# Two attention layers in one kernel: every values group in split form, sums seeded by copies, values four steps behind the scores

## The reference, cut to what matters

```python
# layer 0: 64 inner channels, no scale
g, theta, phi = g_w @ x + g_b, theta_w @ x + theta_b, phi_w @ x + phi_b
y = softmax(theta.T @ phi, axis=-1) @ g.T
x = W_w @ y.T + W_b[:, None] + x
# layer 1: 128 channels
q, k, v = Wq @ x + bq, Wk @ x + bk, Wv @ x + bv
out = softmax((q.T @ k) / sqrt(128), axis=-1) @ v.T
x = x + out.T
```

## Time and profile before

| | us |
|---|---|
| median of the runs | 3249.24 |
| the profiled execution | 3248.75 |
| its span, first to last instruction | 3246.9 |
| TensorE matmuls busy | 3207.7 (99%) |
| GpSimd busy | 3025.7 (93%) |
| VectorE, ScalarE busy | 2091.7, 1897.9 |
| granted TensorE clock | 0.997 |

### The profile page before, as it was taken

How to read it: one execution, slowest core, us unless ns; L and a number is a source line. 1 busy time by engine, 2 the same in 40 slices (tenths; PEclk the granted TensorE clock), 3 DMA queues, 4 the chain that set the end, 5 groups by cost and what they waited for, 6 DMA issues and landing times. The chain is left out here.

```text
span 3246.9 us, 38831 instructions
## 1 busy us (share of the span) xinstructions
PE 3207.7 (99%) x13636; PEld 2198.4 (68%) x13636; DVE 2091.7 (64%) x3036; ACT 1897.9 (58%) x2473; POOL 3025.7 (93%) x1611
## 2 busy tenths in 40 slices
PE   8999999999999999999999999999999999999997
PEld 5555555557777775555777776555577777777775
DVE  5555555556777765555777776555577777777773
ACT  5555555556666655555666665555566666666665
POOL 6988999999999999999999999999999999999998
PEclk9999999999999999999999999999999999999999
DMA  1000000004665650000565664000067575657566
GB/s 52 26 21 26 23 27 26 27 23 94 136 137 117 145 103 27 27 27 27 104 142 119 139 134 101 17 26 27 27 132 141 119 147 115 126 120 144 120 136 120
DMA packets 91922, 271.45 MB, mean 84 GB/s; under 512 B 10192, under 2 KB 10192, under 8 KB 91728
## 3 DMA queue, kind: packets, MB, share of 16 engines
q0 software_dynamic: 55296, 201.35, 32.3%
q1 hardware_dynamic: 36432, 67.62, 6.8%
HBM read 50.83 MB, written 16.78 MB: 21 GB/s over the span
## 5 line engine op out<-in xcount | busy, mean ns | idle before, releaser
L924 DVE TENSOR_REDUCE piece_max<-rough 128x1 f32<-128x512 f32 x2032 | 1316.5, 684 | 707.0 <-PE rough L510 696.9
L1046 POOL TENSOR_TENSOR p_lo<-probs,p_hi 128x1024 fp32r<-128x1024 f32 x448 | 1225.2, 2803 | 54.6 <-ACT probs L835 47.3
L385 POOL TENSOR_TENSOR sums<-sums,probs 128x1024 f32<-128x1024 f32 x448 | 1068.4, 2385 | 108.9 <-ACT probs L841 67.9
L841 ACT ACTIVATE probs<-scores 128x1024 f32<-128x1024 f32 x512 | 521.2, 1024 | 653.9 <-PE scores L539 652.7
L941 DVE TENSOR_TENSOR probs<-scores,shift_rows 128x1024 f32<-128x1024 f32 x512 | 626.6, 1224 | 409.2 <-PE scores L545 406.0
L834 ACT ACTIVATE p_hi<-probs 128x1024 fp32r<-128x1024 f32 x448 | 474.8, 1060 | 552.2 <-DVE probs L941 552.0
L510 PE MATMUL rough<-keys_a,qry_a 128*128 128x512 f32 x2032 | 715.1, 418 | 7.6 <-POOL keys_a L1046 5.9
L835 ACT ACTIVATE probs<-probs 128x1024 f32<-128x1024 f32 x512 | 535.4, 1046 | 88.7 <-DVE probs L941 88.7
L510 PEld LDWEIGHTS rough<-keys_a,qry_a 128*128 128x128 f32 x2032 | 366.2, 188 | 265.6 <-DVE piece_max L924 135.8
L1089 POOL DMA_DIRECT2D sent_sums<-probs x384 | 475.1, 1237 | 0.5 <-issue 0.3
L541 PE MATMUL scores<-qry_a,keys_a 128*128 128x512 f32 x1024 | 446.1, 436 | 0.0
(11 more groups left out here) (94 smaller groups left out, 3177.8 us busy)
## 6 DMA issues: line engine op xcount, KB each, us to landing
sent_sums<-probs POOLq DMA_DIRECT2D x384, 512.0 KB, 5.1
x_q<-x SPq DMA_DIRECT2D x32, 256.0 KB, 2.7
x_res<-x SPq DMA_DIRECT2D x32, 256.0 KB, 3.0
mid<-mid_new SPq DMA_DIRECT2D x32, 256.0 KB, 2.2
x_kv<-mid SPq DMA_DIRECT2D x32, 256.0 KB, 2.7
x_q<-mid SPq DMA_DIRECT2D x32, 256.0 KB, 2.8
x_res<-mid SPq DMA_DIRECT2D x32, 256.0 KB, 4.6
out<-result SPq DMA_DIRECT2D x32, 256.0 KB, 3.5
```

Of the source, the lines that this page charges most:

```text
L385: eng.tensor_tensor(sums[:], sums[:], probs[:, slot(st, s)], ALU.add).then_inc(s_plus, 1)
L841: nc.scalar.activation(probs[:, slot(st, s)], scores[:, s % 2], ACT.Exp, scale=SCALES[0]).then_inc(s_whole, 1)
L924: nc.vector.reduce_max(piece_max[:, t, c:c + 1], src, AX.X).then_inc(s_reduced, 1)
L1046: nc.gpsimd.tensor_tensor(dst, w, rd(hi), ALU.subtract).then_inc(done, 1)
```

## The change

All sixteen groups are split: `WHOLE`, `v_vals`, `value_group` and the seeds go. The first two groups of a block are copied into the accumulators by DMAs of SP (`copy_probs`, `COPIED`), and `sent_sums` is doubled, one pair for odd and one for even blocks. `LAG` is 4; `p_hi` has five places and `p_lo` three, counted on through the stage, and GpSimd now waits for the values of s - 3 before it writes `p_lo` of s. For groups 14 and 15 the send stands ahead of the split. The query's low part is made by VectorE from PSUM right after block and copy, in place of ScalarE's whole copy and GpSimd's subtraction; the pieces wait for it. `take_output` moves to step 4 after a layer 1 block. The moves of v shift to three in the last block of stage 6 and five in the first of stage 7, all eight split. `diag` and `sums` share memory with other tiles.

```diff
-HI_SLOTS = (2, 3, 0, 1)
-LAG = 3
+HI_SLOTS = (2, 3, 4, 0, 1)
+LO_BUFS = 3
+LAG = 4
-TAKE_AT = 3
+TAKE_AT = (3, 4)
-MOVES_AT = ({6: 0, 8: 1, 10: 2, 12: 3, 14: 4}, {1: 5, 3: 6, 5: 7})
-Q_LO_AT = 9
+MOVES_AT = ({6: 0, 9: 1, 12: 2}, {5: 3, 7: 4, 9: 5, 11: 6, 13: 7})
-WHOLE = (2, 3)
-SEED_AT = {2: 0, 3: 2}
-SENT = tuple(range(4, 16))
+COPIED = (0, 1)
...
+            def copy_probs(st, s):
+                sp.wait_ge(s_whole, whole_of(st.g, s))
+                if s == COPIED[0]:
+                    sp.wait_ge(s_fold, st.g - (st.prev == 1))
+                settle(sp)
+                sp.dma_start(sent_sums[:, st.parity, s], probs[:, slot(st, s)]).then_inc(s_copied[s], 16)
...
@@ values (TensorE)
-                if s >= LAG and st.layer == 1 and s - LAG in WHOLE:
-                    if st.opens:
-                        pe.wait_ge(h_v, st.b * BLOCKS + WHOLE_CHUNK + 1)
-                    value_group(st, s - LAG)
-                elif s >= LAG and st.layer == 1:
-                    halved_values(st.b, st.opens, st.g, st.nth, st.parity, s - LAG)
+                if s >= LAG and st.layer == 1:
+                    halved_values(st.b, st.opens, st.g, st.nth, st.parity, st.groups_before, s - LAG)
...
@@ piece (TensorE)
                         pe.wait_ge(h_q, st.g + 2)
                         if st.prev is None:
                             pe.wait_ge(s_diag, st.g + 1)
+                            pe.wait_ge(l_q, st.g + 2)
+                    if m == 1:
+                        pe.wait_ge(l_q, st.g + 2)
...
@@ block_program (ScalarE)
-                    if s == GROUPS - 1 and st.next_q:
-                        take_q_whole(st.g + 2, st.next_q[0], two_banks(1))
...
+                    if s == GROUPS - 1 and st.next_q:
+                        act.wait_ge(s_scores, (st.g + 1) * GROUPS)
+                        take_q_hi(st.g + 2, st.next_q[0], st.parity, two_banks(1))
                     if st.layer == 0:
                         probs_direct(st, s)
...
@@ (VectorE)
+            def split_q(g, layer, parity, src):
+
+                dve.wait_ge(h_q, g + 1)
+                nc.vector.scalar_tensor_tensor(out=qry_b[:, parity], in0=src, scalar=(TH_B, Q_B)[layer],
+                                               in1=rd(qry_a[:, parity]), op0=ALU.add,
+                                               op1=ALU.subtract).then_inc(l_q, 1)
...
+                if st.next_q:
+                    split_q(st.g + 2, st.next_q[0], st.parity, two_banks(1))
...
@@ (GpSimd)
             def split_probs(st, s):
                 pool.wait_ge(s_whole, whole_of(st.g, s))
-                lo_part(p_lo[:, s % len(HI_SLOTS)], probs[:, slot(st, s)], hi_part(s), s_p_lo)
+                if s >= LO_BUFS:
+                    pool.wait_ge(s_used, used(st.g, s - LO_BUFS))
+                elif st.prev == 1:
+                    pool.wait_ge(s_used, used(st.g - 1, s + GROUPS - LO_BUFS))
+                lo_part(low_part(st.groups_before + s), probs[:, slot(st, s)], hi_part(st.groups_before + s), s_p_lo)
...
@@ block_program (GpSimd)
-                    if st.layer == 1 and s in HALVED:
+                    if st.layer == 1 and s >= GROUPS - TPG:
+                        send(st, s)
+                    if st.layer == 1:
                         split_probs(st, s)
-                    if st.layer == 1 and s in SENT:
+                    if st.layer == 1 and s not in COPIED and s < GROUPS - TPG:
                         send(st, s)
-                    if st.layer == 1 and s in SEED_AT:
-                        seed(st, SEED_AT[s])
-                    if s == Q_LO_AT and st.nxt is not None:
-                        split_q(st.g + 1, 1 - st.parity)
```

More of the change, by code:

```diff
@@ L112, in build @@
     assert all(GROUPS == len(a) and sum(a) == PIECES for a in PIECES_AT)
-    assert BLOCKS == 8 and LAG == 3 and GROUPS == 2 * P_BUFS
+    assert BLOCKS == 8 and LAG == 4 and GROUPS == 2 * P_BUFS
     ADDS = GROUPS - 1
@@ L220, in build @@
         s_fold = sem("s_fold")
-        s_seed = sem("s_seed")
-        s_sent = [sem(f"s_sent_{n}") for n in range(TPG)]
+        s_copied = [sem(f"s_copied_{n}") for n in COPIED]
+        s_sent = [[sem(f"s_sent_{m}_{n}") for n in range(TPG)] for m in range(2)]
         s_join = sem("s_join")
@@ L357, in shifted, with fold @@
             return nth * GROUPS + s + 1
-        def fold(eng, layer, g, nth):
+        def fold(eng, layer, g, nth, parity):
             if layer == 0:
@@ L577, in value_batch @@
                     last.then_inc(s_used, 1)
-            def value_group(st, s):
-                pe.wait_ge(s_whole, whole_of(st.g, s))
-                for h in range(TPG):
-                    p = probs[:, slot(st, s), h * QB:(h + 1) * QB]
-                    last = mm(acc_out[:, st.parity], cols(v_vals, s % TPG * TPG + h, KT), p,
-                              start=False, stop=False)
-                last.then_inc(s_used, 1)
             def values(st, s):
                 if s < LAG and st.prev == 1:
-                    halved_values(st.prev_b, False, st.g - 1, st.prev_nth, 1 - st.parity, GROUPS + s - LAG)
+                    halved_values(st.prev_b, False, st.g - 1, st.prev_nth, 1 - st.parity, st.prev_groups_before,
+                                  GROUPS + s - LAG)
                 if s == BATCH_AT and st.prev == 0:
@@ L759, in scaled, with take_q_hi @@
                 return nc.scalar.activation(dst, src, ACT.Copy, scale=scale)
-            def take_q_whole(g, layer, src):
+            def take_q_hi(g, layer, parity, src):
                 act.wait_ge(p_q, g + 1)
-                if not (isinstance(g, int) and g == 0):
-                    act.wait_ge(l_q, g)
-                copy(q_whole[:], src, (TH_B, Q_B)[layer])
-            def take_q_hi(layer, parity, src):
                 copy(qry_a[:, parity], src, (TH_B, Q_B)[layer]).then_inc(h_q, 1)
@@ L799, in move_v @@
                 act.wait_ge(h_hold, c + 1)
-                copy(v_vals[:] if c == WHOLE_CHUNK else v_hi[:, v_chunk(c)], held(c)).then_inc(h_v, 1)
+                copy(v_hi[:, c], held(c)).then_inc(h_v, 1)
             def shift_to_row(layer, g, parity):
@@ L1031, in block_program @@
                         m += 1
-                    if s == V_LO_AT and st.stage.prepares == "kv" and st.i != WHOLE_CHUNK:
+                    if s == V_LO_AT and st.stage.prepares == "kv":
                         split_v(st.stage.made * BLOCKS + st.i, st.i, acc_out[:, 1 - st.parity])
+                if st.next_q:
+                    split_q(st.g + 2, st.next_q[0], st.parity, two_banks(1))
                 if st.ends:
-                    fold(dve, st.layer, st.g, st.nth)
+                    fold(dve, st.layer, st.g, st.nth, st.parity)
                     reciprocals(st.g, st.parity)
```

169 lines of the change are left out of this document (73 added, 96 removed).

## The result

The changed kernel takes 3297.56 us, median of four runs (3296.55 to 3300.78), against 3249.4 for the kernel before on the same chip: a ratio of 1.015 (95% interval 1.0132 to 1.0167), 48 us. The forecast was 3248, its range ended at 3266.

What follows compares the result with a forecast made beforehand. TensorE bounds the kernel, GpSimd close behind in layer 1 and, after the change, bounding the last two images there. Phi stages -7.2, last two images +6.4, start -0.7 sum to -1.5 us: 3248, range 3231 to 3266.

Steps and rivals of the forecast that it cites:

- TensorE's ledger: Layer 1 blocks: two whole value groups out, two split groups in, gain 0.72 us each; TensorE asks 55.88, 55.0, 54.1.
- 0.4 for the form: Possible TensorE cost of leaving the fp32 form after the denominators, 0.4 us, cutting the gain to 0.39 a block.
- rival C: TensorE in layer 1: split groups bring the form change, gain only 0.39 us a block; 3253; chance 0.07.
- GpSimd's ledger: Layer 1 blocks: seeds and query's low half out, two splits and sends in, net +0.5 us; 55.5 a phi block.
- the margin: End of a layer 1 block: the fold ends 1.6 us ahead of the denominators, which GpSimd may lose over eight blocks.
- the forecast's chain to the fold: GpSimd from the end of values(9): splits 12 to 15, 0, 1, four sends, 0.6 of wait, fold; ends 1.6 us ahead.
- The new wait: GpSimd at send(14), until send(12) lands: 0.6 us a block, within 0.3 to 1.6, and 0 in late blocks.
- rival B: Ring of sends decides: 1.6 us or more of wait at send(14) each block; 3272, 3257 to 3280; chance 0.21.
- The key chunk: Phi stage's end: last chunk's split on GpSimd comes later, TensorE's 1.47 us wait grows by 2.2, to 3 to 4.
- The last two images: Layer 1 of the last two images, with GpSimd as the bound: +6.4 us in sum.
- the two terms: Last block and tail: fold to last split 46.4 us (+3.3), from there to the denominators 3.4 (-3.3).
- A: Only TensorE's gain holds, the fold is never late: about 3233, 3226 to 3241; chance 0.24.

Runs made afterwards that it cites:

- E3: Changed kernel without any GpSimd sends, so the denominators lack 14 of 16 groups; 3216.45 us.
- E15: Changed kernel, last two sends behind their splits, SP's copies after the last landing, phi's low half on VectorE from PSUM; 3252.86 us.
- E1: Changed kernel with the last two sends of a layer 1 block behind their splits again; 3276.02 us.
- E4: Kernel before with only sends 14 and 15 put ahead of their splits; 3267.69 us.
- E6: Changed kernel with the last two sends behind their splits and SP's whole copies waiting for the last landing; 3260.17 us.
- E7: Kernel before with values four steps behind, five high and three low buffers, take_output at step 4 after layer 1 blocks; 3264.7 us.
- E12: Kernel before with the query's low half on VectorE, values four steps behind, five high and four low buffers; 3247.16 us.
- E16: Changed kernel with only phi's low half moved to VectorE, read from PSUM; 3282.86 us.
- E8: Kernel before with the query's low half on VectorE and ScalarE's whole copy gone; 3245.07 us.
- E2: Changed kernel with SP's two copies a block cut to 64 of 1024 columns; 3297.47 us.
- E11: Kernel before with the low halves of the query, and of phi and k in layer 1 stages, on VectorE; 3246.74 us.
- E9: Changed kernel, last sends behind splits, copies after the last landing, low halves of phi and k on VectorE; 3287.72 us.

## Why the prediction was wrong

**TensorE's ledger: right.** 55.9, 55.0, 54.1 in E3, so 0.7 less a block and no 0.4 for the form (rival C is out). The records of L584 start 0.43 apart, so a whole group of four is the 1.72 by itself.

**GpSimd's ledger and the margin: right in the numbers.** 55.56 of work against 55.5; the fold 1.70 ahead against 1.6. E3 lacks the sends that the forecast's chain to the fold held, so it does not test that chain; E15, with the sends in place, has the same 1.71 in 14 of 16 phi blocks.

**The new wait: the step that failed.** It was put at one wait, at send(14), of 0.6 a phi block, within 0.3 to 1.6, and 0 in late blocks. Measured: 1.31 there, 0.57 at send(15), 0.25 at send(8), 2.13 in all, outside the bounds. So the step failed twice over: the wait was too short, and two of the three waits were not in it. Three errors in it. The landing came 4.06 after send(12)'s end, not 3.9: 0.16. (I took the landing after the end as a difference of medians and of extremes, 3.6, 3.9 and 4.9; send by send the trace of before has 3.55, 3.66 and 6.03, so the upper bound was too low.) GpSimd starts 0.56 and 0.75 us after a landing that it waits for, where I had it start at once; that alone doubles the wait. And send(15) depends on send(13) in the same way and was left out: even a landing 0.18 before GpSimd was free (1779.74 against 1779.92) did not spare it 0.57. In late blocks send(14) waits at most 0.26 in six of eight, as forecast, but send(15) 0.88 to 1.04 in five, and the sends of a block 1.1 to 2.3 in seven. So the cycle was 57.7 and not 56.1, 1.8 over TensorE's 55.9, which uses up the margin of 1.7 in one block; from then on nearly every denominator waits for its fold, the mark named for rival B (phi blocks over 56.6). E1 and E4 price the order of the two sends: 21.5 and 19 us. Taken off one after the other from after's 3297.6, the order gives 21.5 (E1), the copies that then count 15.9 (E6), and phi's low half on VectorE 7.3 (E15): 44.7 of the 48.

**The key chunk: mis-sized.** Forecast a wait of 3 to 4 (1.47 + 2.2), at the most 5.4. TensorE's gap was 3.26 and 4.46 in the rows of after and E7, up to 5.2, as said; what was left out is what follows: GpSimd, out of low buffers, waits for the values behind that gap, twice, and TensorE soon falls to half clock. E3 has the same loop without any send (2.22 of TensorE's wait, then 3.75 and 1.85 of GpSimd's), at 4 us a block. The two blocks cost 6.1 + 6.3 = 12.4 over before, not 4.4. E7, and after beside E12, show that it is the third buffer in place of the fourth, and E15 and E16 that it takes the chunk's split on GpSimd as well: with that on VectorE three buffers do. I had reckoned them as a delay of release in the steady state and not as a loop that a pause goes round in.

**The last two images: the same wait.** Forecast +6.4, measured 7.6 + 15.0 + 4.1 = 26.7. In the tail the two terms were near: last fold to last split 46.7 (forecast 46.4), from there to the denominators 3.9 (3.4); the last fold came 3.2 us later in its block than before. The 15.0 of the last image lie in its second to sixth block: 61.6 in the second, behind the five low halves of v that GpSimd makes in the first, then 55.1 to 59.5, where before has 54.8 and TensorE's ledger is 54.1.

**The clock: not in the sum.** Behind some of TensorE's pauses its granted clock is 1.2 and not 2.4 GHz, which the forecast gave no price. Engine totals of after around the end of stage 2, then of E7 (last three columns: clock granted, DMA share, GB/s):

```profile
1181.00:1184.00 3.00, 0.85 (x4) 0.72 (x5) 0.46 (x2) 2.00 (x2) 2.09 (x2) 1.00 0.84 162
1184.00:1187.00 3.00, 3.00 (x13) 2.57 (x11) 0.97 (x2) 0.00 (x0) 0.84 (x1) 0.54 0.31 60
```

```profile
1176.00:1181.00 5.00, 0.84 (x4) 0.37 (x2) 1.90 (x2) 3.20 (x4) 5.00 (x4) 0.95 0.68 131
1181.00:1184.00 3.00, 2.71 (x6) 2.15 (x7) 1.29 (x2) 0.00 (x0) 0.24 (x1) 0.50 0.68 131
1184.00:1187.00 3.00, 3.00 (x12) 2.69 (x11) 0.00 (x0) 0.00 (x0) 1.78 (x1) 0.50 0.00 0
```

Between the start and the tail such stretches add up to 0 us in before, 41.0 in after (11 of them), 37.5 in E1, 20.5 in E6, 13.7 in E7, 6.8 in E3 and 0 in E8. At half clock split matmuls start 0.43 apart and not 0.23, so 41.0 us hold some 20 of lost TensorE time. How much of the 48 that is, no run shows by itself: where the fold is late anyway, a slower TensorE is partly hidden. It need not be much: E4's 19 us come with a single stretch of 3.4 us, and E2's trace has 54.6 us of them at the time of after.

**Rivals.** B had the mechanism (landings set GpSimd's cycle) but named other causes, the copies and the query's load, and a price of 3272, too low for the second wait and the key chunk. E2 clears the copies in this kernel. The query's load is untested; send(12), beside it, lands 4.1 after its end in the median where sends 2 to 5 take 3.6, so what it can be charged with is up to 0.5 a block. A needed a GpSimd that is never late; 3216 without sends and 3253 in E15 show that its ledger was there and its condition was not. The Trainium skill (DMA: Bandwidth & Descriptors, Anatomy of one DMA) gives an estimate of 3.2 us for such a transfer, by which send(14) would never wait; no send of after lands sooner than 4.4 us after its dispatch (median 5.4, most 8.6), and the measurement decides.

## What to carry to other kernels

Moving a DMA ahead of work in a queue also moves the next user of its buffer ahead: count every pair that shares a buffer, take the landing from its end send by send, its median and its largest, and add what the engine needs to start again. A buffer taken from a ring is to be priced in the block with the longest pause, not in the steady one. With two engines level, 1 us of wait a block is not 1 us: once the margin is used up it is paid in every block, and a pause of TensorE can halve its clock for a stretch besides. An operation moved to VectorE should keep one input in PSUM where GpSimd is busy.

## What was not expected of the hardware

GpSimd started a DMA 0.56 to 0.75 us after the landing that it waited for, in all 58 waits of after, and spent 0.57 even where the landing was 0.18 before it was free. Between the wait and the DMA its program has one instruction, a semaphore increment (`settle`); what share of the time is its, no run shows.

After pauses of 3.3 and 4.5 us of TensorE the granted clock was half for about 3 and 6 us (0.54 in 1184 to 1187 of after; 0.50 from 1181 to 1187 in E7). Shorter pauses did it too, and not always: in after it fell behind one of 0.97 (which ended at 2661) and not behind one of 1.84 (which ended at 1735).

VectorE's subtraction of 512 columns took 680 ns with one input in PSUM, 674 ns with both in SBUF where GpSimd's subtraction was at its end (E11), and 2.6 to 8.2 us with both in SBUF beside one (E9), ending 0.55 us after GpSimd's each time. The Trainium skill (SBUF — State Buffer, Who interferes with whom) says that a VectorE operation with two SBUF inputs contends with a GpSimd instruction that reads SBUF. The trace agrees, and here it was VectorE that waited, in four of the 24 even though its record starts 0.3 to 0.4 us ahead of GpSimd's.
